# Norms of a six-block decoder: the order of squares and scalings on VectorE

## The reference

```
x = layernorm(x + attn(x))      # six times, with a different block each time
layernorm(x) = (x - mean) / sqrt(var + eps)                     # mean and var over the 128 features
rmsnorm(x)   = x * rsqrt(mean(x*x) + eps) * w
layer_norm with gain and bias = (x - mean) * rsqrt(var + eps) * g + b
```

## The kernel before

| norm | first square at us | mean | scaling | what comes next |
|---|---|---|---|---|
| 1 | 40.57 | no | L203 | residual sum, VectorE L357 |
| 2 | 53.77 | yes | L201 | norm 3, whose means wait for all four batches |
| 3 | 64.52 | yes | L206, L210 | cross attention: context projections L511 and L517, copied by ScalarE L588 and L592 |
| 4 | 676.40 | yes | L201 | self attention: projections L774, VectorE L923 |
| 5 | 948.89 | yes | L206, L210 | expert network: router L1085, which waits for the last batch |
| 6 | 1083.15 | yes | L206, L210 | residual sum L357 |
| 7 | 1096.55 | yes | L201 | norm 8 |
| 8 | 1105.97 | no | L203 | delta rule, VectorE L1343 and L1348 |
| 9 | 1484.15 | no | L203 | gated feed-forward, L1207, which waits for the last batch |
| 10 | 1528.94 | yes | L201 | cross attention L1595, which waits for the last batch |
| 11 | 1596.12 | yes | L201 | norm 12 |
| 12 | 1604.40 | no | L203 | self attention, L774 |
| 13 | 1838.60 | no | L203 | expert network, L1747, which waits for the last batch |
| 14 | 2045.10 | yes | L201 | the four stores of the output, L1891 |

## Time and profile before

### The profile page before, as it was taken

How to read it: one execution, slowest core, us unless ns; L and a number is a source line. 1 busy time by engine, 2 the same in 40 slices (tenths; PEclk the granted TensorE clock), 3 DMA queues, 4 the chain that set the end, 5 groups by cost and what they waited for, 6 DMA issues and landing times.

```text
span 2055.8 us, 23221 instructions
## 1 busy us (share of the span) xinstructions
PE 1599.0 (78%) x7584; PEld 735.5 (36%) x7584; DVE 1424.8 (69%) x2595; ACT 891.7 (43%) x1856; POOL 478.0 (23%) x599
## 2 busy tenths in 40 slices
PE   6799999999999699997995300222397599988998
PEld 2345544545454222222441000222333245533443
DVE  7477766677676678875547999999757677744343
ACT  2466555565565156664334301122133156654332
POOL 0000000000000212112780475444203123103443
PEclk8899999999999789999997655555599789989999
DMA  4000000000000322300000000000100222200000
GB/s 176 1 1 1 1 1 1 1 1 1 1 1 1 80 59 68 104 2 1 0 0 0 0 0 0 1 0 1 61 0 0 71 69 86 50 1 1 0 0 21
DMA packets 19618, 44.54 MB, mean 22 GB/s; under 512 B 3820, under 2 KB 12844, under 8 KB 18732
## 3 DMA queue, kind: packets, MB, share of 16 engines
q1 hardware_dynamic: 18156, 40.31, 6.6%
q10 hardware_dynamic: 1344, 2.75, 0.6%
HBM read 33.02 MB, written 9.44 MB: 21 GB/s over the span
## 4 chain that ended last, share of the span: by engine, by line
PE 65%; DVE 25%; ACT 4%; issue 4%; DMA 1%; POOL 1%; SPq 0%; ACTq 0%; POOLq 0%; DVEq 0%
PE ps L493 7%; PE ps L459 7%; PE ps L787 5%; PE ps L471 5%; PE ps L807 5%; PE ps L826 5%; DVE arena L1435 4%; PE ps L443 3%; PE ps L1092 3%; PE ps L1207 3%; PE ps L1208 3%; PE ps L1103 3%; DVE arena L1427 3%; PE ps L1215 2%; DVE arena L1442 2%
## 5 line engine op out<-in xcount | busy, mean ns | idle before, releaser
L953 DVE TENSOR_REDUCE stat<-ps 128x1 f32<-128x512 f32 (+3 forms) x512 | 279.5, 582 | 96.4 <-PE ps L811 47.5
L882 ACT ACTIVATE arena<-ps 128x512 f32<-128x512 f32 (+3 forms) x512 | 247.2, 515 | 149.6 <-PE ps L826 76.7
L575 ACT ACTIVATE arena<-ps,stat 128x544 f32<-128x544 f32 x256 | 180.6, 710 | 220.6 <-DVE stat L614 220.6
L1549 PE MATMUL ps<-cent,reg 128*128 128x64 f32 x256 | 56.7, 407 | 279.8 <-POOL cent L1479 265.0
L614 DVE TENSOR_REDUCE stat<-ps 128x1 f32<-128x544 f32 x256 | 173.6, 720 | 145.1 <-PE ps L459 144.2
L807 PE MATMUL ps<-arena 72*128 72x512 bf16 (+3 forms) x512 | 184.0, 367 | 35.6 <-DMA arena<-b_parts 30.8
L826 PE MATMUL ps<-arena 75*128 75x512 bf16 (+3 forms) x512 | 179.3, 354 | 8.1 <-ACT arena L882 5.7
L459 PE MATMUL ps<-arena 64*128 64x272 f32 x1024 | 155.0, 422 | 13.4 <-ACT arena L575 11.7
L493 PE MATMUL ps<-arena 128*64 128x512 f32 (+1 forms) x640 | 158.0, 606 | 6.1 <-DVE arena L634 5.4
L1336 ACT ACTIVATE arena<-arena 128x32 f32<-128x32 f32 x128 | 45.0, 352 | 258.1 <-DVE arena L1442 187.6
L1549 PEld LDWEIGHTS ps<-cent,reg 128*128 128x128 f32 x256 | 55.2, 332 | 282.0 <-issue 138.9
(11 more groups left out here) (290 smaller groups left out, 2950.4 us busy)
## 6 DMA issues: line engine op xcount, KB each, us to landing
arena<-b_parts SPq DMA_DIRECT2D x168, 96.0 KB
b_parts<-arena SPq DMA_DIRECT2D x64, 128.0 KB, 1.8
reg<-wM_dram SPq DMA_DIRECT2D x1, 3072.0 KB, 10.2
arena<-b_parts ACTq DMA_DIRECT2D x24, 96.0 KB
reg<-wB_dram SPq DMA_DIRECT2D x1, 2048.0 KB, 12.2
reg<-wM_dram SPq DMA_DIRECT2D x1, 2048.0 KB, 16.8
reg<-wD_dram SPq DMA_DIRECT2D x1, 1913.0 KB, 11.4
wF_sb<-wF_dram SPq DMA_DIRECT2D x1, 1476.0 KB, 20.6
```

The costliest lines, as they stand in the source:

```text
L575: e.activation(prob_of(P, r).rearrange("p (a k) -> p a k", a=2), score_banks(r), ACT.Exp, bias=x_neg[:, at_:at_ + 1], accum_out=x_sums[:, ...
L882: e.activation(p_t[:, m % 8, q0:T], ps[:, S1 + m % S2, q0:T], ACT.Exp).then_inc(exp_done, 1)
L953: e.tensor_reduce(nm[:, G % 2, u // 4, u % 4:u % 4 + 1], ps[:, step % S1, 0:keys(u)], AX.X, ALU.max, negate=True).then_inc(max_done, 1)
```

## The change

`dve` runs over n from 0 to N+1 and issues the squares of batch n, and then the scaling of batch n-2. The two helpers take a batch number; what they issue for one batch is unchanged, waits included. For four batches VectorE's order goes from

```diff
             def dve(self, e):
-                self.dve_squares(e)
-                self.dve_scale(e)
-
-            def dve_squares(self, e):
-                for n, (src, dst, w, slot) in enumerate(self.chunks):
-                    c = src
...
-            def dve_scale(self, e):
-                for n, (src, dst, w, slot) in enumerate(self.chunks):
-                    c = self.tmp(cent, n) if self.mean else src
...
+                N = len(self.chunks)
+                for n in range(N + 2):
+                    if n < N:
+                        self.dve_squares(e, n)
+                    if n >= 2:
+                        self.dve_scale(e, n - 2)
+
+            def dve_squares(self, e, n):
+                c = src = self.chunks[n][0]
+                if self.mean:
+                    c = self.tmp(cent, n)
+                    e.wait_ge(sem("norm_mean"), self.first_mean + n + 1)
...
+            def dve_scale(self, e, n):
+                src, dst = self.chunks[n][0:2]
+                c = self.tmp(cent, n) if self.mean else src
+                e.wait_ge(sem("norm_dev"), self.first + n + 1)
...
-            n_ctx.dve_squares(e)
+            for n in range(len(n_ctx.chunks)):
+                n_ctx.dve_squares(e, n)
...
-            n_ctx.dve_scale(e)
+            for n in range(len(n_ctx.chunks)):
+                n_ctx.dve_scale(e, n)
```

More of the change, by code:

```diff
@@ new lines, in dve @@
+                for n in range(N + 2):
[8 more added lines that the diff above has]
+                    e.wait_ge(sem("norm_mean"), self.first_mean + n + 1)
+                    e.tensor_tensor(c, src, ps[:, self.chunks[n][3], 0:self.chunks[n][2]],
+                                    ALU.subtract).then_inc(sem("norm_cent"), 1)
+                    e.wait_ge(sem("norm_cent"), self.first_mean + n + 1)
+                else:
+                    e.wait_ge(*self.ready[n])
+                if self.first:
+                    e.wait_ge(sem("norm_done"), self.first)
+                e.tensor_tensor(self.tmp(dev, n), c, c, ALU.mult).then_inc(sem("norm_sq"), 1)
@@ new lines, in dve_scale @@
+            def dve_scale(self, e, n):
+                src, dst = self.chunks[n][0:2]
+                c = self.tmp(cent, n) if self.mean else src
+                e.wait_ge(sem("norm_dev"), self.first + n + 1)
+                if self.gain is None:
+                    e.tensor_tensor(dst, c, self.tmp(dev, n), ALU.mult).then_inc(sem("norm_done"), 1)
+                elif self.bias is None:
+                    e.scalar_tensor_tensor(out=dst, in0=c, scalar=v(self.gain), in1=self.tmp(dev, n),
+                                           op0=ALU.mult, op1=ALU.mult).then_inc(sem("norm_done"), 1)
+                else:
+                    e.scalar_tensor_tensor(out=self.tmp(cent, n), in0=c, scalar=v(self.gain),
+                                           in1=self.tmp(dev, n), op0=ALU.mult,
+                                           op1=ALU.mult).then_inc(sem("norm_scaled"), 1)
+                    e.wait_ge(sem("norm_scaled"), self.scaled + n + 1)
+                    e.tensor_scalar(dst, self.tmp(cent, n), v(self.bias), None,
+                                    ALU.add).then_inc(sem("norm_done"), 1)
```

## The result

The change makes the kernel slower: 2062.80 us (median of 15 runs, 2057.36 to 2069.68) against 2056.36 for the kernel before, run beside it (15 runs, 2052.16 to 2060.90). The ratio is 1.0033, interval 1.0020 to 1.0046, so 4.1 to 9.5 us more. The forecast was a loss of 3.7 us and 2057.6, with a range to 2061.0: the direction is right, the size too small. 2.4 us of the distance to 2062.8 are the base (the first three runs of the kernel before had a median of 2053.94, all fifteen 2056.36); the rest is size, 6.8 where 3.7 was worked out (ratio times base; the two medians are 6.4 apart). Either of the two alone would have left the time inside the range.

What follows compares the result with a forecast made beforehand. In a norm VectorE, TensorE and ScalarE all take part, none full; ScalarE's Ln and Exp chain leads to the last scaling. Terms 2.00 + 0.39 + 0.98 + 0.31 = 3.68 us on 2053.94 gave 2057.6, range 2054.3 to 2061.0.

Steps and rivals of the forecast that it cites:

- The bound and the mechanism: Norm 11: sc0 ahead pushes sq3 back 0.64 to 0.65 us against a slack of 0.25, costing 0.40 us.
- Norms 3 and 7: Norm 3, with gain and bias, costs 0.98 us; norm 7, opening at the lower clock, costs 0.39 us.
- Early results: Rival: sc0 starts 1.29 us earlier; if stages behind eight norms waited for batch 0, 10.4 us less, 2043.5; chance 5%.
- swallowed the delay: Rival: transfers or GpSimd work behind the norms hide the delay; half the sum swallowed gives 2055.8 us; chance 18%.
- Norm 5: Norm before the router, which waits for batch 3's scaling: costs 0.31 us.
- Norm 7 and the like: Norms with a mean and no gain: 0.39 us in norm 7, 0.40 each in norms 2, 4, 10, 11 and 14.
- the norms without a mean: Norms 1, 8, 9, 12 and 13 cost 0, hidden by slow variance matmuls; all at full clock, an estimated 0.19 us each.
- 0.1 left: Norm 13, where the clock rises midway: matmul ready for Ln at 1845.44, Ln 3 was at 1845.56, so cost 0.
- The clock: Rival: one or two more openings at the lower clock, 2059.7 to 2061.8 us, 15%; one fewer, 2055.5, 7%.

Runs made afterwards that it cites:

- fill_swap: The changed kernel plus 5 to 13 useless TensorE matmuls behind the last variance of nine norms; 2056.34 us, ratio 0.9991 to the kernel before.
- fill: The kernel before, old order, plus 5 to 13 useless TensorE matmuls behind the last variance of nine norms; 2049.01 us, ratio 0.9967.
- the chains: Kernels with 24 further norms with a mean behind norm 14; without useless matmuls or held-back square, old order 2310.15 us, new order 2368.85.
- chain_old: The kernel before plus 24 further norms with a mean behind norm 14, all in the old order; 2310.15 us.
- again: The changed kernel timed once more against the kernel before; 2062.47 us, ratio 1.0036.
- lag1: Against the kernel before, scaling of batch n-1 follows the squares of batch n in all fourteen norms; 2097.34 us, ratio 1.0209.
- mean_only: Against the kernel before, the new order only in the nine norms with a mean; 2063.58 us, ratio 1.0039.
- rms_only: Against the kernel before, the new order only in the five norms without a mean; 2060.46 us, ratio 1.0016.
- delay: The kernel before, old order, with one or two useless squares ahead of batch 3's square in norms with a mean; 2057.79 us, ratio 1.0009.

## Why the prediction was right and wrong

**The bound and the mechanism were right.** sc0 right behind sq2, sq3 0.63 later (0.64 to 0.65 forecast), slack of about 0.2, and 0.42 us per norm for 0.40: all read from the slack of one square. Norms 3 and 7 came as worked out (1.01 and 0.42, for 0.98 and 0.39). Early results paid nowhere; nothing swallowed the delay either.

**Small terms were off.** Norm 5 has 0.37 for 0.31. Norm 7 and the like lose 0.42, for 0.39 and 0.40. For the norms without a mean I gave 0, and 0.19 as an estimate for full clock; fill_swap against fill shows 0.31 and 0.30 there in norms 8 and 12. The 0.49 of norm 13 is not all the order: its Exp 0 to Exp 3 is 3.77 to 4.68 in six traces with the old order in it and 4.51 to 4.65 in four with the new one. "0.1 left" was a cover read at one setting of the clock, and the clock there varies. Without the norms that lack a mean the schedule comes to 2.52 + 1.01 + 0.37 = 3.9 us, where 3.68 was forecast.

**The step that failed is the rival "The clock".** I wrote that one or two more openings could fall to the lower level, priced them at 2.1 us each from 5.47 against 3.36, and gave this 15%, with 7% for one fewer, as if it were drawn by lot and on average next to nothing; the sum has nothing for it. It is partly drawn by lot, but the change loads the lot. Means over the four traces of the new order against the three or four of the old one, from the table: norm 3 +1.57 (4.30 less 2.73), norm 7 +0.68 (4.21 less 3.53), block 5 +0.59 (59.91 less 59.32). Norm 6 gives 0.34 back (first Exp at 2.70 against 3.04). Together 2.5 us. The two expert networks belong to the same account, by the same means: behind norm 5 -1.2 (123.8 less 125.0), behind norm 13 +0.6 (199.1 less 198.5). With them it is 1.9 us, and with the schedule's 3.9, 5.8 us; 6.8 were timed, 4.1 to 9.5. The whole traces can't check such a sum: the stage between norms 12 and 13 alone takes 217 to 227 us from one trace to the next. That a term of this sign is missing is shown by norm 3 and the chains; its size in this kernel, some 2 to 3 us, is an estimate. This term, which came on top of the sum and not beside it, should have stood in it. The price of 2.1 us for one opening was too high: those above cost 0.6 to 1.9 us each.

The Trainium skill, page "TensorE: Matmul & The Clock Gate", section "A second HAM failure mode: psum-queue depth-cycling", has a like case, a bf16 kernel that cycles through PSUM banks: TensorE idles briefly and often between groups of matmuls, and its clock swings between the two levels. The chains agree with that (0.96 down to 0.80 by one wait of 0.7 us more in each norm). The page finds the loss between the bursts; here it is in the matmuls themselves, 960 ns instead of 601 for a pass of the means of norm 3. I had drawn only the variation between runs from that page. That part holds too, as block 5 of chain_old shows, and it let me take the matter for pure chance.

**A second reading gives a like split, but not its places.** Over the 135 timed runs of again, lag1, mean_only, rms_only, delay, fill and fill_swap and of the kernel before beside them, inside each kernel, a run with a mean granted clock higher by 0.001 is 1.06 us shorter. Moved to the same clock along this line, the change (again) is 4.9 us slower than the kernel before, mean_only 5.6, rms_only 0.9, delay 2.1, fill_swap over fill 5.2. So some 4 to 5 us are the order itself, and some 2 to 2.5 us go with a lower clock. The line is rough: for lag1 it gives 31 where the norms of its trace are 37.5 us longer. Nor does it say where the clock is lost: rms_only's mean clock is 0.0026 below the kernel before, as much as that of the change (0.0022) and of mean_only (0.0024), though its norms 3 and 7 and block 5 open as in the old order. What stays open: how the missing 2 to 3 us divide over the stages; whether the norms without a mean and the stage behind norm 13 add anything in the whole kernel (rms_only's interval begins at 0.2 us); why the stage behind norm 5 is shorter; and what keeps blocks 3 and 6 low for long stretches.

## What to carry to other kernels

Before moving an instruction that waits for a late result ahead of one that feeds another engine, read the slack of the latter in the timeline: here 0.2 us, and all beyond it was paid in every norm. Then look at what the wait handed to TensorE does to the stage behind it, above all in a row of short stages, where it stands idle a good part of the time anyway: an added wait there belongs in the sum, priced by what the next stage's first matmuls cost at the other clock. And where TensorE has to wait in any case, useless matmuls in that wait can be worth more than a better order: 6.8 us here, from some 90 of them.

## What the runs showed of the hardware

- The gap right before a stage does not tell its clock. Norm 3 opened at full clock behind a wait of 2.88 us in the old order and low behind one of 2.26 in the new; what differed is a wait of 0.92 us some 3.4 us earlier, before the last variance of norm 2. lag1, with waits of 1.77 and 0.80 us there, opened norm 3 almost at full clock (3.10), so no rule follows from it.
- The eight fp32 passes of 128x512 of norm 8 take 6.39 us opened low and 3.67 opened at full clock; of the 2.72 us the norm gets 1.89. ScalarE's pairs, 1.24 us apart, then set its pace.
- A scaling whose input is long there follows a 128x512 tensor_tensor after 0.61 us, in the old order and in the new.
- Nine useless 128x128 fp32 matmuls per norm in the chain raise TensorE's busy time in 230 us from 169.84 to 213.15, and take the mean distance of its norms from 10.62 to 10.18 us, 10.6 us over the 24; the whole kernel, with those ahead of the chain, is 12 to 14 us shorter.
